# Products that nobody reads in three waits of TensorE, and the gates' operations moved behind the first rounds

## The reference

```python
mod = (silu(c) @ wmod).reshape(1, 6, 1, -1)
sa, ca, ga, sb, cb, gb = (mod[:, i] for i in range(6))
ga = (2 * (ga >= 0) - 1) * maximum(abs(ga), 0.25)     # the gates; gb in the same way
h = layernorm(x) * (1 + ca) + sa
x = x + ga * attn(h)
h = layernorm(x) * (1 + cb) + sb
x = x + gb * ffn(h)

def attn(x):                       # 16 heads of 16
    q = einsum('bnhd,hed->bnhe', heads(x), Wq)
    attn = softmax(einsum('bnhe,bmhe->bhnm', q, q) * 4)
    return einsum('bhnm,bmhe->bnhe', attn, q).reshape(B, N, D) @ Wp.T + bp

def ffn(x):                        # weights are integers with a scale for each 128 rows
    h = layernorm(x) * ln_gamma + ln_beta
    return x + 0.5 * (silu(h @ w1 + b1) @ w2 + b2)    # 256 -> 1024 -> 256
```

## Time and profile before

| what | us |
|---|---|
| median of 3 runs (lowest, highest) | 2063.98 (2062.30, 2064.37) |
| the profiled execution | 2063.12 |
| its span in the trace | 2061.3 |
| ScalarE busy | 1937.2 (94%) |
| TensorE busy | 1891.8 (92%) |
| VectorE busy | 1181.1 (57%) |
| mean granted clock of TensorE | 0.992 of full speed |

### The profile page before, as it was taken

The page is one execution under the profiler, slowest core; times in us unless marked ns, Lnnn a source line. Parts: engine busy times, 40 slices in busy tenths (PEclk is TensorE's granted clock), DMA queues, the critical chain, the costliest instruction groups (busy, mean ns, idle before and its releaser), DMA issues.

```text
span 2061.3 us, 42981 instructions
## 1 busy us (share of the span) xinstructions
PE 1891.8 (92%) x18325; PEld 532.4 (26%) x18325; DVE 1181.1 (57%) x1620; ACT 1937.2 (94%) x1502; POOL 1.3 (0%) x6
## 2 busy tenths in 40 slices
PE   5788889999999999999999999999999999999997
PEld 3311112222222222222222222222222222222224
DVE  7546445655575555755456555755557554565544
ACT  3799999999999999999999999999999999999982
POOL 0000000000000000000000000000000000000000
PEclk9899999999999999999999999999999999999998
DMA  5541111121111112111211111112111112111100
GB/s 161 142 133 36 46 47 45 46 57 41 51 41 51 51 44 59 41 47 44 56 47 49 52 41 54 38 51 51 47 56 45 47 41 56 46 40 41 31 12 12
DMA packets 121344, 108.11 MB, mean 52 GB/s; under 512 B 21936, under 2 KB 120112, under 8 KB 120896
## 3 DMA queue, kind: packets, MB, share of 16 engines
q1 hardware_dynamic: 120400, 103.69, 18.8%
q10 hardware_dynamic: 752, 1.67, 0.2%
HBM read 96.49 MB, written 8.65 MB: 51 GB/s over the span
## 4 chain that ended last, share of the span: by engine, by line
ACT 76%; issue 13%; PE 6%; DVE 1%; ACTq 0%; DVEq 0%
ACT attend_probs L788 41%; ACT attend_probs L793 33%; ACT attend_half_tanh L774 2%; PE attend_sums L839 2%; PE attend_scores L827 2%; PE attend_scores L847 1%; PE attend_out L847 1%; PE attend_out L853 0%; ACT attend_ffn_in L799 0%; PE attend_scores L853 0%; DVE attend_st L1204 0%; DVE z L1216 0%; DVE attend_probs L1008 0%; PE attend_sums L853 0%; DVE attend_rsqrt_work L139 0%
## 5 line engine op out<-in xcount | busy, mean ns | idle before, releaser
L788 ACT ACTIVATE attend_probs<-attend_scores 128x2048 f32<-128x2048 f32 x704 | 1326.0, 1883 | 34.4 <-PE attend_scores L827 34.4
L1008 DVE COPY attend_probs<-attend_scores 128x1024 f32<-128x1024 f32 x672 | 822.6, 1224 | 687.0 <-PE attend_scores L827 676.6
L839 PE MATMUL attend_sums<-attend_probs,values 128*17 128x512 f32 x8192 | 1011.1, 597 | 0.0
L793 ACT ACTIVATE attend_probs<-attend_probs 128x1024 f32<-128x1024 f32 x672 | 743.6, 1106 | 1.6 <-DVE attend_probs L1008 1.6
L827 PE MATMUL attend_scores<-asks,keys 64*128 64x512 f16 x4096 | 566.6, 380 | 125.2 <-ACT attend_probs L788 98.3
L827 PEld LDWEIGHTS attend_scores<-asks,keys 64*128 64x128 f16 x4096 | 149.5, 94 | 757.9 <-ACT attend_probs L788 615.4
L839 PEld LDWEIGHTS attend_sums<-attend_probs,values 128*17 128x17 f32 x8192 | 171.8, 96 | 499.3 <-issue 459.2
L847 PE MATMUL attend_out<-w,hidden 128*32 128x256 f32 x1920 | 124.2, 379 | 0.0
L847 PE MATMUL attend_out<-attend_ffn_in,w 128*32 128x512 f32 x896 | 116.6, 592 | 0.0
L847 PEld LDWEIGHTS attend_out<-w,hidden 128*32 128x32 f32 x1920 | 62.0, 110 | 86.3 <-issue 64.2
L1097 DVE TENSOR_SCALAR attend_half_in<-attend_out,b_col 128x512 f32<-128x512 f32 x56 | 42.0, 751 | 52.0 <-PE attend_out L847 52.0
(11 more groups left out here) (141 smaller groups left out, 512.6 us busy)
## 6 DMA issues: line engine op xcount, KB each, us to landing
keys<-parts_dram SPq DMA_DIRECT2D x768, 64.0 KB
keys<-parts_dram SPq DMA_DIRECT2D x256, 56.0 KB
asks<-parts_dram SPq DMA_DIRECT2D x192, 64.0 KB
start_x_in<-L_attn_x SPq DMA_DIRECT2D x8, 512.0 KB, 9.5
parts_dram<-start_q_parts SPq DMA_DIRECT2D x16, 256.0 KB, 2.6
attend_x_now<-L_attn_x SPq DMA_DIRECT2D x8, 512.0 KB, 4.3
out<-base SPq DMA_DIRECT2D x16, 256.0 KB, 2.5
asks<-parts_dram SPq DMA_DIRECT2D x64, 56.0 KB
```

The costliest lines, as they stand in the source:

```text
L788: act.activation(place(gg, r, 0, both), ps_scores[:, 0:2 * both, :], ACT.Exp, scale=scale).then_inc(exps_done, 1)
L793: act.activation(place(gg, r, 2), place(gg, r, 2), ACT.Exp, scale=scale).then_inc(exps_done, 1)
L839: last = pe.matmul(ps_sums[32 * hq:32 * hq + E1, :], values[:, j + STEPS * b, (gg % Q_GROUPS) * Q_HEADS + hq, :], place(gg, r, Q_HEADS * j ...
L1008: dve.tensor_copy(place(gg, r, 2), ps_scores[:, 4:6, :]).then_inc(copied, 1)
```

## The change

A helper `keep_running` multiplies the identity by itself, 128 by 128, a given number of times into a PSUM area that is free at that moment. Its result is read by nobody. It is called in three places of TensorE's list: 22 products in round g = 2 of the first stage, between q by features and the turn of group 3; 14 products behind the modulation vector, after a wait for `v_copied` (the copy of the last values, which frees the bank); and 40 products in the tail, between the projection and the wait for `z2_ready`. The gates' seven operations on VectorE no longer stand ahead of the loop: they are cut in four portions, `modulation(0)` to `modulation(3)`, which run behind the copies of rounds 4 to 7 of step 0.

```diff
+def keep_running(pe, bank, operand, times):
+
+    for _ in range(times):
+        pe.matmul(bank, operand, operand, start=True, stop=True)
...
                     last.then_inc(q_feat_mm, 1)
+                    if g == 2:
+                        keep_running(pe, ps_turn[:, 0, 0:P], ident[:, :], 22)
                     if g + 1 < G:
                         turn(g + 1)
...
                     last.then_inc(mod_mm, 1)
+                pe.wait_ge(v_copied, G)
+                keep_running(pe, ps_qt[:, 0, 0:P], ident[:, :], 14)
 
                 pe.wait_ge(fits_ready, 1)
...
                     project(t, [ps_scores[:, 2, :], ps_out][t // 2][:, (t % 2) * D:(t % 2 + 1) * D])
+                keep_running(pe, ps_scores[:, 3, 0:P], ident[:, :], 40)
                 for half in range(2):
...
-                dve.wait_ge(mod_copied, 2)
                 gates = mod[:, 0:4:3, :]
-                dve.tensor_scalar(sign, gates, 0.0, 2.0, ALU.is_ge, ALU.mult).then_inc(mod_step, 1)
-                dve.tensor_scalar(negated, gates, -1.0, None, ALU.mult).then_inc(mod_step, 1)
-                dve.wait_ge(mod_step, 2)
-                ...
+
+                def modulation(part):
+
+                    if part == 0:
+                        dve.wait_ge(mod_copied, 2)
+                        dve.tensor_scalar(sign, gates, 0.0, 2.0, ALU.is_ge, ALU.mult).then_inc(mod_step, 1)
+                        dve.tensor_scalar(negated, gates, -1.0, None, ALU.mult).then_inc(mod_step, 1)
+                    elif part == 1:
+                        dve.wait_ge(mod_step, 2)
+                        dve.tensor_scalar(sign, sign, -1.0, None, ALU.add).then_inc(mod_step, 1)
+                        dve.tensor_tensor(negated, negated, gates, ALU.max).then_inc(mod_step, 1)
+                    elif part == 2:
+                        dve.wait_ge(mod_step, 4)
+                        dve.scalar_tensor_tensor(out=gates, in0=negated, scalar=0.25, in1=sign, op0=ALU.max, op1=ALU.mult).then_inc(mod_step, 1)
+                        dve.tensor_scalar(mod[:, 2, :], mod[:, 2, :], 1.0, None, ALU.add).then_inc(mod_step, 1)
+                    else:
+                        dve.wait_ge(mod_step, 6)
+                        dve.tensor_scalar(sign[:, 0, :], mod[:, 3, :], 0.5, None, ALU.mult).then_inc(mod_step, 1)
+                        dve.wait_ge(mod_step, 7)
...
+                        if gg == 0 and 4 <= r < 8:
+                            modulation(r - 4)
                         if gg == 1 and 4 <= r < 12:
                             weights(r - 4)
```

## The result

The changed kernel takes 2056.08 us (median of 7 runs, 2054.98 to 2056.44) against 2063.88 us for the kernel before (7 runs beside them, 2062.0 to 2064.37). The ratio is 0.9964, with a 95% interval from 0.9952 to 0.9975, so the kernel is faster by 0.36%. The forecast was 2056.6 us. The profiled execution took 2056.44 us, its span is 2054.7 us, and the mean granted clock rose from 0.992 to 0.998.

A forecast was written before the change was run, and what follows sets the result against it. ScalarE's exponentials set the pace (76% of the chain); outside them TensorE runs cold behind three waits. Savings of 2.4 + 1.9 + 3.1 = 7.4 us from the median 2063.98 gave 2056.6 us, range 2054.0 to 2059.5.

The forecast's parts named there:

- The rate of a product: An f32 product by a 128-column operand on TensorE takes two records, 0.236 us at 2.4 GHz.
- First stretch: First stage: 22 products behind round g = 2 keep the clock up and delay nothing; 2.4 us saved.
- Second stretch, TensorE last: Stage end behind the modulation vector: the 14 products might make TensorE last to the meeting; 0.1 us lost.
- Rival (b): End of the stage: TensorE comes last, reading the flag only behind the products; 1.2 us more, 2057.8 us; chance 0.10.
- The gates: Loop start: moving the gates' VectorE operations lets the copy run earlier, so the second round starts 1.4 us earlier.
- the warm first round: First round of scores: its first two pairs run at 2.4 GHz, saving 0.4 us.
- The clock in the first rounds: First rounds: the clock falls all the same and the third round stays mostly cold; only 0.2 us saved.
- Rival (a): First rounds: the clock holds, so the third round's 1.9 us go too, not 0.2; 2054.9 us; chance 0.18.
- Third stretch: Tail: 40 products keep the turn of z2 and the up products warm, less 0.2 us delay; 3.1 us saved.
- (c): One of the two long fills misses, in the last the clock falls or it runs over; 2059.7 us; chance 0.09.
- (d): All three fillings: products don't count as work for the clock, the last fill becomes the bound; 2070.9 us; chance 0.04.
- (e): Whole kernel: the profile's clock isn't where the time is, only the gates count; 2062.5 us; chance 0.03.

The follow-up runs named there:

- e8: The changed kernel with 24 products instead of 14 behind the modulation vector; 2057.61 us.
- e1: The kernel before with only the gates' operations moved and none of the products added; 2062.21 us.
- e6: The changed kernel with the 22 and the 40 products replaced by 44 and 80 transposes, the 14 products kept; 2055.80 us.
- r9: The changed kernel run once more, unaltered; 2054.81 us.
- e3: The kernel before with only the 14 products behind the modulation vector added, with their wait; 2063.33 us.
- e5: The changed kernel with 7 more products behind the scores of rounds 0 and 1 of step 0; 2054.03 us.
- e7: The changed kernel with 20 products in the tail instead of 40; 2058.76 us.
- e12: The changed kernel with 31 products in the tail instead of 40; 2057.71 us.
- r10: A repeat of e5: the changed kernel with 7 more products behind the scores of rounds 0 and 1; 2054.39 us.
- e4: The kernel before with only the 40 products of the tail added; 2059.67 us.
- e2: The kernel before with only the 22 products in round g = 2 of the first stage added; 2060.63 us.

## Why the prediction was right, step by step

The time was forecast at 2056.6 us and measured at 2056.08, so it is faster, as given 0.88. The mechanism was right; that the number came within 0.5 us is partly luck. By the profiles the sum was 0.5 us too large, and the base of 2063.98, the median of three runs, stands 1.3 to 1.5 us above the medians of the kernel's 66 later runs (2062.5 to 2062.7); the two errors work against each other. By its steps:

- *The rate of a product*, 0.236 us: measured 2 x 0.115 = 0.23. Right, and with it the ends of the three fillings.
- *First stretch*, 2.4 us: 2.33 in the profiled pair, and no delay. As a mean it was 0.6 too large: the profile of before that I read had the longest A of four (32.93; the others 31.94, 32.17, 32.58), so 1.8 us. The lower bound, 0.8, allowed for it, but the term was taken from one execution as if the length of the cold work were fixed. Two slips of the text don't enter the sum: products 5% slower would have run 0.1 us over the release, not 0.3, and the warm twin of the cold work stands one round later, not two.
- *Second stretch, TensorE last* (0.1): right that it isn't last. The products ended at 79.40 and SyncE's last load at 79.84; e8 shows what happens beyond. Rival (b) is out.
- *The gates* (1.4) and *the warm first round* (0.4): together 1.8 expected up to the second exponential. Measured 0.33 + 1.71 = 2.04 in the pair. Of the 1.71, the gates gave 1.42, as e1 shows (3.01 us between the exponentials, not 4.43); the other 0.29 are the second round's scores, still warm, which I hadn't in the sum. They don't come in each execution: in e6 and r9 the clock fell before these scores, and the distance is 3.01. B is shorter by 0.4 (8.98 on the mean of five without the 14 products, 8.56 of eight with them, e8 aside), and C by 1.5 (11.78 of four, 10.24 of seven). With the portions behind rounds 4 to 7, VectorE was idle for 0.55 us before a copy at the tightest; no copy was late. e3 adds what I hadn't said: the 0.4 us depend on the gates' move.
- *The clock in the first rounds*: forecast to fall in spite of the short waits, and it did, just ahead of the third round's scores (0.50 from 85.1). The term of 0.2 was -0.6 in the profiled pair, since the fourth round waited 2.12 us, and about 0 on the mean. Rival (a), 0.18, did not come, and e5 shows that it was a matter of filling two more waits. The Trainium skill's rule on long waits between bursts (TensorE: Matmul & The Clock Gate, "Why this matters for your kernels") would have given rival (a): the trace doesn't bear it out, for waits of 1.23 and 1.75 us and 1.1 us of a third, with 0.82 us of work between them, were enough.
- *Third stretch*, 3.1 us: 3.25 in the pair, 3.15 on the mean of D (23.33 without, 20.18 with). Right, and the 0.2 us of delay did not come, since the records ran at 0.115 us: they ended after 9.20 us, and e7 and e12 show the release at 9.19 and 9.20.
- Rivals (c), (d) and (e): no filling missed; (d) fell with the granted clock of 1.00 under all three, and even transposes hold it; (e) is out by A and D.

The sum was 7.4; the parts by the table give 1.8 + 0.4 + 1.5 + 3.15 = 6.9, and the spans of the pair 6.6. The medians lie 7.8 and 7.7 us apart. The last 0.8 to 1 us isn't located; it is within what the starts of the executions scatter, and the seven runs of before beside the changed kernel have a median 1.2 to 1.4 us above those of its 66 others.

## What to carry to other kernels

Where TensorE waits for a chain of another engine and is itself the bound just behind the wait, the cold work behind it is a cost of its own, and idle products can buy it back; size them so that they end at the release, from the rate of the same shape in the trace, and check which engine comes last to any meeting behind them. Don't judge a wait by its own length: short waits with little work between them brought the fall here as a long one did, and a filling that left 2 us open was worth nothing in the profile and in most executions. Small work that stands ahead of a loop's first operation on an engine can be the bound of the loop's start, though the engine is idle for half of each later round: products that made the first scores earlier gained nothing until that work was moved.

## What the runs showed of the hardware

- The length of a single wait doesn't decide whether and when the clock falls. In the first stage the kernel before got through a wait of 3.7 us, and r10 fell 1.3 us behind one of 3.67. In e1 the clock held through 4.55 us and fell 0.7 us into the work behind. In the same wait of 5.3 us ahead of the turn of group 3 the fall came 2.8 us after its start in e4, 3.5 in before, 4.9 in e3 and 5.4 in e1.
- A fall with only short waits: e12 fell with waits of 2.01 and 1.14 us around 1.08 us of work in its profile, and, by their mean granted clock, not in three of its other executions.
- Runs of one kernel differ by where the clock falls and by the start: the turn of group 3 stood between 40.20 and 42.65 us in the first eight experiments, because the second group of tokens, 512 KB, landed sooner or later (its moments start at 8.97 us in e4, at 9.90 in e2, at 10.99 in before, and the turn comes 31.2 us behind them in all three).
- The attention itself has two lengths. From the eleventh round to the last, the same instructions took 1886.03 us in the profiles of before, e2 and e6 (1886.02 to 1886.04), and 1886.56 to 1886.60 in the eleven others. It makes up nearly all of the -0.56 of the account above; the change has no part in it, since both kinds hold kernels with it and without. Its cause isn't known.
